# A ring of 64 pairs of gathered tiles in place of 32, laid over queries and table, with the experts' weights loaded after the gathers

## The chip, the core and the metric

The kernel runs on one core of one Trainium2 chip. Its engines are PE (matrix products), DVE and ACT (element by element), POOL (here mostly the issuer of indirect DMAs) and SP (here the issuer of plain DMAs and a counter of semaphores). The metric is device time in microseconds (us), lower is better. Of each kernel one further execution was profiled; all times inside the kernel come from it.

## What is computed

One layer over a graph of 6,250 nodes with 256 features and 206,250 edges (src, dst), sorted by dst. The parts that matter here, cut from the reference:

```python
x = h @ W                                   # 256 -> 64
el, er = x @ Wl.T, x @ Wr.T                 # 4 heads each
e = exp(leaky_relu(el[src] + er[dst], 0.2))
rowsum = segment_sum(e, src)
heads = [segment_sum((e / rowsum[src])[:, hd:hd+1] * x[dst], src) for hd in range(4)]
gnn = elu(stack(heads, axis=1) + b).reshape(N, 256)

x = x + gnn + linear_attention(layernorm(x))   # x here is the layer's input
x = x + moe(layernorm(x))                      # 8 experts, top 2, each 256 -> 256 -> 256
```

## The kernel before

Nodes are laid out in 49 tiles of 128. The kernel has four stages.

**Projections and sort.** PE and ACT project every tile to queries (q_all), keys, values and a row of the gather table tb (four er values, 64 features and a one: GW = 69 words). SP stores tb to HBM as gather_table. DVE meanwhile sorts all edges by src in SBUF; the attention runs beside the sort, and POOL adds its result to base in four chunks. At the end dst_x holds the sorted edges' dst and src_f their src.

**The edge loop.** The sorted edges form 806 pairs of tiles (NP; GT = 2 tiles of 128 edges in a pair). Nodes are cut into 196 windows of 32, and an item is a pair seen from one window. Items number 1,001, in groups of four: 251 groups (NG). DVE works out tables of which pair and window each item has, ACT sends them through HBM into registers' reach (trow), and every engine then runs a loop, four groups to a turn, with the pair and the window read into registers.

- POOL (lines 1548 to 1558) isn't looped: for every pair p it waits until pair p - 8 has been told ready (LAND = 8) and, from p = RING on, until pair p - RING is free, then issues two indirect DMAs, each of which gathers 128 rows of 276 bytes into gat.
- SP (watch, lines 1624 to 1637) goes through the pairs in order. It waits until pair p has landed and raises s_ready (L1627); then, from p = BEHIND on, it waits until the group that last uses pair p - BEHIND has been aggregated (s_agg) and raises s_free (L1636). With RING = 32, LAND = 8, BEHIND = 24 the same step of SP serves both of POOL's waits.
- ACT locates group g (L1392, waits for s_ready), copies the turned one-hots of group g - 1 from PSUM to hotT (L1382, waits for PE) and takes the exponential of group g - 3 (L1376).
- DVE makes one-hots (L773), sums and slopes the logits of group g - 2 (L754 to L768), weighs the one-hots of group g - 3 (L778) and adds up group g - 5 (L789).
- PE aggregates group g - 4 with 16 products from gat (L1145), spreads el of group g - 1 (L1135) and turns the one-hots of group g (L1127).

In its first eight groups ACT also issues load_expert: two DMAs of 256 KB each for one of the eight experts, the weights w1_s and w2_s (L1368, L1369). After its last group it issues two loads of biases (L1425).

**After the loop.** SP waits for all sums and issues, for each of seven tile groups, 16 small copies (L1646) that permute acc into moved. DVE averages (L832 to L836), ACT's exp_low (L1430) follows, then ELU, a second layernorm and the routing.

**Experts.** PE, ACT and DVE run the two-layer experts over slots of 128 tokens. Both PE and DVE first wait for s_ew, the landing of all weights and biases.

SBUF's large tensor is the arena, in which stages lie over each other by word offsets: q_all at 0 and tb at A_TB = 6272; src and dst of the edges from A_E = 9653; the two key buffers and right of the sort from A_K = 12981 to A_END1 = 17973. In the edge loop gat lay at A_K (32 x 138 words) and share_w behind it at A_S; the experts' weights lie at 0 to A_B = 8192, so over q_all and part of tb, which were free by then; hotT lay at A_B.

Of the kernel before, what the change touches and what calls it, by code (L numbers as in the profile page):

```python
# [10 lines left out]
BF16 = mybir.dt.bfloat16  # L11

P = 128
# [109 lines left out]
def gps_layer(nc, x, src, dst, W, Wl, Wr, gnn_b, w_qkv, mem_kv, w_out, b_out, g_out, g_pre,  # L123
# [3 lines left out]
    HD, C = Wl.shape  # L127
    _, MH, MD, MEM = mem_kv.shape
    HID = MH * MD
    NE, _, F = w1.shape  # L130
    T = -(-N // P)
    TAIL = N - (T - 1) * P
    SCALE = float(MD) ** -0.5
    KC = D // P
# [19 lines left out]
    GT = 2  # L154
    WN = 32
# [5 lines left out]
    GS = GI * GT  # L161
    NG = -(-NI // GI)
    RING, LAND, BEHIND = 32, 8, 24
    HOTS, UNROLL = 4, 4
    GW = HD + C + 1
    AW = C + 1
    SPL = 3 * HD + 1
# [16 lines left out]
    with ExitStack() as ctx:  # L184
        def sb(name, shape, dt=F32):
            return ctx.enter_context(nc.sbuf_tensor(name, shape, dt))
# [33 lines left out]
        A_E = A_TB + T * GW  # L220
        A_K = A_E + 2 * n_sort
        A_END1 = A_K + 3 * n_sort
        A_W1, A_W2 = 0, NE * KC * F
        A_B = A_W2 + NE * KC * D
        A_F = A_B + 2 * NE * D
        A_END2 = A_F + 2 * TS * RW + 12 * D
        A_G = A_K
        A_S = A_G + RING * GT * GW
        arena = sb("arena", [P, max(A_END1, A_END2, A_S + 2 * GS * P)])
# [8 lines left out]
        w1_s = arena[:, A_W1:A_W2].rearrange("p (e k f) -> p e k f", e=NE, k=KC)  # L238
        w2_s = arena[:, A_W2:A_B].rearrange("p (e k f) -> p e k f", e=NE, k=KC)
# [9 lines left out]
        assert A_F <= A_G  # L249

        spare = arena[:, A_END1:A_S + 2 * GS * P]
# [3 lines left out]
        o_el = T * 6 + (KC + 1) * P  # L255
        el_all = spare[:, o_el:o_el + T * HD].rearrange("p (t h) -> p t h", t=T)
        el3 = spare[:, o_el + T * HD:o_el + T * HD + -(-T * SPL // 2)].bitcast(BF16)[:, 0:T * SPL].rearrange("p (t c) -> p t c", t=T)
        assert o_el + T * HD + -(-T * SPL // 2) <= A_S + 2 * GS * P - A_END1
# [50 lines left out]
        gat = arena[:, A_G:A_S].rearrange("p (r w) -> p r w", r=RING)  # L309
        share_w = [x.rearrange("p (s h n) -> p s h n", s=GS, h=HD) for x in ring(A_S, 2, GS * P)]  # L310
        hot = [x.rearrange("p (s n) -> p s n", s=GS) for x in [rows_b.rearrange("p a c -> p (a c)").bitcast(BF16)[:, i * GS * WN:(i + 1) * GS * WN] for i in range(HOTS)]]
        hotT = [arena[0:WN, A_B + i * GS * P // 2:A_B + (i + 1) * GS * P // 2].bitcast(BF16).rearrange("p (c e) -> p c e", c=GS) for i in range(2)]
        assert A_B + GS * P <= A_E
# [51 lines left out]
        s_tab = sem("s_tab")  # L365
        s_ksub = sem("s_ksub")
        s_kexp = sem("s_kexp")
        s_qTp = sem("s_qTp")
# [4 lines left out]
        s_arow = sem("s_arow")  # L373
# [18 lines left out]
        s_agg = sem("s_agg")  # L392
        s_acc = sem("s_acc")
        s_ew = sem("s_ew")
# [869 lines left out]
        def _(act):  # L1264
# [98 lines left out]
            def load_expert(e):  # L1363

                if e == 0:
                    act.wait_ge(s_tab, 16)
                    act.wait_ge(s_qTp, T)
                act.dma_start(w1_s[:, e, :, :], w1[e].rearrange("(k p) f -> p k f", p=P)).then_inc(s_ew, 16)  # L1368
                act.dma_start(w2_s[:, e, :, :], w2[e].rearrange("(k p) f -> p k f", p=P)).then_inc(s_ew, 16)  # L1369

# [24 lines left out]
            def group(g, u):  # L1395

                now = g if isinstance(g, int) else NG // 2
                if u == 0:
                    values = items_of(act, "tile", g)
                    for v in range(UNROLL):  # L1400
                        place["tile", v] = values[v * GI:v * GI + GI]
                if now < NG:
                    locate(g, u)
                if 1 <= now < NG + 1:
                    copy_hot(g - 1, (u - 1) % UNROLL)
                if 3 <= now < NG + 3:
                    weights(g - 3, (u - 3) % UNROLL)
                if isinstance(g, int) and g < NE:
                    load_expert(g)
            assert NE <= 2 * UNROLL  # L1410
# [11 lines left out]
            for g in range(NG, NG + 3):  # L1422
                group(g, g % UNROLL)
            for rows, d in ((b1_b, b1), (b2_b, b2)):
                act.dma_start(rows.rearrange("p e f -> p (e f)"), d.rearrange("e f -> (e f)").partition_broadcast(P)).then_inc(s_ew, 16)  # L1425
# [85 lines left out]
        def _(pool):  # L1511
# [34 lines left out]
            pool.wait_ge(s_tab, 16)  # L1546

# [174 lines left out]
```

## Time and profile before

| | us |
|---|---|
| three runs | 3670.96, 3671.51, 3678.86 (median 3671.51) |
| profiled execution | 3671.64 |
| its span, first to last instruction | 3669.9 |
| first gather starts | 633.7 |
| last gather starts | 3069.8 |
| last aggregation ends | 3115.8 |

The span and the time of the profiled execution differ by 1.7 us. In the views an engine's busy time is that of its own instructions; DMAs that it issues, register loads and semaphore waits don't count. PE's matrix products and PEld's weight loads overlap. Where a view names a releaser, it is inferred from semaphore events; "remote" and "another core or an unknown queue" mean that none was found, and "issue" means time in which the engine waited for nothing that the profile shows. POOLq, SPq and ACTq are the engines' own instruction queues. The granted clock (PEclk) is a share of 2.4 GHz.

### The profile page before, as it was taken

How to read it: one execution, taken by the hardware profiler on the slowest of the kernel's cores; microseconds unless marked ns; L12 is line 12 of the kernel's file. 1: busy time of each engine (PE TensorE's matmuls, PEld its weight loads, DVE VectorE, ACT ScalarE, POOL GpSimd, SP SyncE). 2: the span in 40 equal slices, each digit the busy share in tenths (PEclk: the TensorE clock that was granted, in tenths of full speed). 3: DMA queues.
4: the chain of work that ended last, by engine and by line, in shares of the span. 5: the costliest groups of instructions: out<-in, count | busy, mean ns of one | idle time of the engine just before them, and what ended most of it. 6: DMA issues, size and time to landing. Idle time of an engine off the chain costs nothing.

```text
span 3669.9 us, 48930 instructions
## 1 busy us (share of the span) xinstructions
PE 1914.9 (52%) x10823; PEld 1641.5 (45%) x10824; DVE 1677.2 (46%) x5067; ACT 918.6 (25%) x2670; POOL 1845.4 (50%) x1844
## 2 busy tenths in 40 slices
PE   3824551154554455545555455545554557358874
PEld 1423331054544445444444444545444446247663
DVE  6788899233333333333333333333333334764343
ACT  3711221121211122112121112112121212564431
POOL 0021133666666666666666666666666662144433
PEclk9856655555555555555555555555555555569997
DMA  8020000211111111111111111111111111224554
GB/s 268 0 21 0 1 0 2 58 41 24 23 24 24 24 23 23 24 24 23 24 23 24 23 24 23 24 24 23 24 23 24 22 24 36 67 92 152 156 161 136
DMA packets 146361, 161.17 MB, mean 44 GB/s; under 512 B 44070, under 2 KB 113818, under 8 KB 146016
## 3 DMA queue, kind: packets, MB, share of 16 engines
q0 software_dynamic: 60992, 82.75, 11.5%
q1 hardware_dynamic: 79668, 70.58, 6.6%
q10 hardware_dynamic: 5612, 6.86, 0.6%
q8 instruction: 29, 0.48, 0.1%
q14 instruction: 60, 0.49, 0.0%
HBM read 101.18 MB, written 52.20 MB: 42 GB/s over the span
## 4 chain that ended last, share of the span: by engine, by line
another core or an unknown queue 42%; PE 21%; DVE 14%; issue 10%; ACT 7%; ACTq 2%; SPq 1%; POOL 1%; DVEq 1%; DMA 1%; POOLq 0%
PE ps L1145 6%; DVE arena L643 5%; DVE arena L642 4%; PE ps L1127 3%; ACT loc L1392 3%; PE ps L1223 3%; PE ps L1239 2%; ACT arena L1382 1%; PE ps L1104 1%; PE ps L1135 1%; ACTq L1392 1%; PE ps L1037 1%; PE ps L1231 1%; DVE arena L660 1%
## 5 line engine op out<-in xcount | busy, mean ns | idle before, releaser
L1557 POOL DMA_INDIRECT arena<-gather_table,arena x1612 | 1524.9, 946 | 928.5 <-issue 436.1
L1145 PE MATMUL ps<-arena 128*128 x4016 | 931.4, 419 | 208.5 <-issue 164.6
L1145 PEld LDWEIGHTS ps<-arena 128*128 128x128 f32 x4016 | 883.3, 329 | 263.5 <-issue 263.2
L1382 ACT ACTIVATE arena<-ps 32x1024 bf16<-32x1024 bf16 x251 | 254.0, 1012 | 1899.6 <-remote 1679.7
L778 DVE TENSOR_TENSOR arena<-rows_b,ps 128x1024 f32<-128x1024 bf16 x251 | 305.6, 1218 | 696.0 <-ACT ps L1376 546.9
L1135 PE MATMUL ps<-el,arena 32*128 x2008 | 115.4, 173 | 964.5 <-ACT arena L1382 843.5
L1135 PEld LDWEIGHTS ps<-el,arena 32*128 32x128 bf16 x2008 | 92.3, 102 | 1001.2 <-issue 981.3
L754 DVE TENSOR_REDUCE zed<-ps 128x32 f32<-128x96 f32 x251 | 64.2, 256 | 826.3 <-remote 756.8
L1127 PE MATMUL ps<-ident_b,rows_b 128*32 128x128 bf16 x2008 | 258.0, 310 | 26.6 <-issue 25.1
L643 DVE TENSOR_TENSOR arena<-arena 128x512 f32<-128x512 f32 (+2 forms) x328 | 248.1, 756 | 0.0
L789 DVE TENSOR_TENSOR big<-ps,big 128x65 f32 x1004 | 226.1, 225 | 46.7 <-issue 5.8
L1392 ACT ACTIVATE loc<-arena,xnx 128x2 f32 x1004 | 212.0, 280 | 105.1 <-issue 82.4
L1569 POOL DMA_INDIRECT slot_rows<-big,el x98 | 106.7, 1088 | 249.7 <-DVE ends_w L925 126.3
L1127 PEld LDWEIGHTS ps<-ident_b,rows_b 128*32 128x32 bf16 x2008 | 193.2, 139 | 37.5 <-issue 25.9
L642 DVE TENSOR_TENSOR arena<-arena 128x512 f32<-128x512 f32 (+2 forms) x328 | 205.3, 626 | 0.6
L1104 PE MATMUL ps<-ident,arena 128*128 128x128 f32 x286 | 61.0, 397 | 218.1 <-DVE arena L643 215.8
L1580 POOL DMA_INDIRECT arena<-expert_rows,el x98 | 93.4, 953 | 141.0 <-DMA expert_rows<-arena 67.7
L760 DVE TENSOR_TENSOR zed<-zed,arena 128x8 f32<-128x8 f32 x1004 | 156.8, 169 | 7.0 <-DVE zed L754 0.3
L1104 PEld LDWEIGHTS ps<-ident,arena 128*128 128x128 f32 x286 | 53.4, 211 | 227.2 <-DVE arena L643 223.2
L1223 PE MATMUL ps<-arena,xnx 128*128 x476 | 131.6, 401 | 22.7 <-issue 14.2
L1239 PE MATMUL ps<-arena 128*128 x476 | 127.1, 391 | 0.0
L1531 POOL TENSOR_TENSOR big<-big,xnx 128x896 f32<-128x896 f32 x7 | 15.7, 2272 | 217.3 <-DVE xnx L582 217.3
(269 smaller groups left out, 2187.1 us busy)
## 6 DMA issues: line engine op xcount, KB each, us to landing
arena<-gather_table,arena POOLq DMA_INDIRECT x1612
arena<-slot_rows SPq DMA_DIRECT2D x119, 128.0 KB
expert_rows<-arena SPq DMA_DIRECT2D x119, 128.0 KB
slot_rows<-ends_w SPq DMA_DIRECT2D x2, 4480.0 KB, 25.7
arena<-big SPq DMA_DIRECT2D x112, 56.9 KB
slot_rows<-ends_w SPq DMA_DIRECT2D x1, 6272.0 KB, 32.9
base<-in_x_dram SPq DMA_DIRECT2D x4, 1536.0 KB
out_dram<-base SPq DMA_DIRECT2D x5, 896.0 KB
```

Of the source, the lines that this page charges most:

```text
L642: dve.tensor_tensor(bl, al, ah, ALU.min if up else ALU.max).then_inc(s_key, 1)
L643: dve.tensor_tensor(bh, al, ah, ALU.max if up else ALU.min).then_inc(s_key, 1)
L778: dve.tensor_tensor(share_w[u % 2], bcast(hot[u % HOTS], 2, HD), bcast(pw, 3, WN), ALU.mult).then_inc(s_share, 1)
L789: dve.tensor_tensor(acc[:, bass.ds(b, 1), :], ps[:, 4 + par:5 + par, i * AW:i * AW + AW], acc[:, bass.ds(b, 1), :], ALU.add).then_inc(s_ac ...
L1127: ins = pe.transpose(out_[:, c * P:c * P + P], hot[u % HOTS][:, c, :], ident_b[:, :])
L1135: ins = pe.matmul(ps[:, 2 + par, c * SPL:(c + 1) * SPL], hotT[par][:, c, :], el4[0:WN, bass.ds(place["el", u][c // GT], 1), :].rearrange(" ...
L1145: ins = pe.matmul(ps[:, 4 + par, i * AW:i * AW + AW], share_w[par][:, i * GT + c, :, :].rearrange("p h n -> p (h n)"), gat[:, bass.ds(plac ...
L1223: ins = pe.matmul(ps[:, 1 + j % 2, 0:F], slot_T[j % 2][:, k, :], w1_s[:, bass.ds(e, 1), k, :].rearrange("p a f -> p (a f)"), start=(k == 0 ...
L1239: ins = pe.matmul(ps[:, 4 + j % 2, 0:D], hidT[j % 2][:, k * P:k * P + P], w2_s[:, bass.ds(e, 1), k, :].rearrange("p a f -> p (a f)"), star ...
L1382: act.activation(hotT[par], ps[0:WN, par, :].bitcast(BF16).rearrange("p (c e) -> p c e", c=GS), ACT.Copy).then_inc(s_hT, 1)
L1392: ins = act.activation(loc[u % 2][:, i * GT:i * GT + GT], src_f[:, bass.ds(place["tile", u][i], GT)], ACT.Identity, bias=bases[:, sl(g * G ...
L1557: pool.indirect_dma_start(gat[:, p % RING, c * GW:(c + 1) * GW], None, table_d, bass.IndirectOffsetOnAxis(ap=dst_x[:, t:t + 1], axis=0)).t ...
```

## The change

RING goes from 32 to 64 and BEHIND from 24 to 56; LAND stays 8. gat moves to the start of the arena, where q_all and tb lay (64 x 138 = 8,832 words, up to A_E at most). share_w moves to A_K, hotT behind it. Since the ring now lies where the experts' weights go, ACT's loads of them leave the first eight groups and stand behind a new wait for the last aggregation, ahead of the biases. POOL's gathers get one more wait, s_arow for all 49 tiles, since q_all is read until then. The early small tensors get their own room behind A_END1.

```diff
-    RING, LAND, BEHIND = 32, 8, 24
+    RING, LAND, BEHIND = 64, 8, 56
...
-        A_G = A_K
-        A_S = A_G + RING * GT * GW
-        arena = sb("arena", [P, max(A_END1, A_END2, A_S + 2 * GS * P)])
+        A_G = 0
+        A_S = A_K
+        N_SPARE = T * 6 + (KC + 1) * P + T * HD + -(-T * SPL // 2)
+        assert A_G + RING * GT * GW <= A_E and A_S + 3 * GS * P <= A_END1
+        arena = sb("arena", [P, max(A_END1 + N_SPARE, A_END2)])
...
-        gat = arena[:, A_G:A_S].rearrange("p (r w) -> p r w", r=RING)
+        gat = arena[:, A_G:A_G + RING * GT * GW].rearrange("p (r w) -> p r w", r=RING)
...
-            def load_expert(e):
-
-                if e == 0:
-                    act.wait_ge(s_tab, 16)
-                    act.wait_ge(s_qTp, T)
-                act.dma_start(w1_s[:, e, :, :], w1[e].rearrange("(k p) f -> p k f", p=P)).then_inc(s_ew, 16)
-                act.dma_start(w2_s[:, e, :, :], w2[e].rearrange("(k p) f -> p k f", p=P)).then_inc(s_ew, 16)
-
...
-                if isinstance(g, int) and g < NE:
-                    load_expert(g)
-            assert NE <= 2 * UNROLL
...
             for g in range(NG, NG + 3):
                 group(g, g % UNROLL)
+            act.wait_ge(s_agg, NG)
+            for e in range(NE):
+                act.dma_start(w1_s[:, e, :, :], w1[e].rearrange("(k p) f -> p k f", p=P)).then_inc(s_ew, 16)
+                act.dma_start(w2_s[:, e, :, :], w2[e].rearrange("(k p) f -> p k f", p=P)).then_inc(s_ew, 16)
...
             pool.wait_ge(s_tab, 16)
+            pool.wait_ge(s_arow, T)
```

## Rows read from the trace of the kernel before

**Rows 1.** The page's first part: each engine's busy time, share and instructions.
```profile
PE 1914.9 (52%) x10823; PEld 1641.5 (45%) x10824; DVE 1677.2 (46%) x5067; ACT 918.6 (25%) x2670; POOL 1845.4 (50%) x1844
```

**Rows 2.** Instructions of one line: ns min/median/max, first and last start in us.
```profile
L1557 POOL DMA_INDIRECT arena<-gather_table,arena x1612: 938/944/2112, 633.7 to 3069.8; - x180
...
L1368 ACTq DMA_DIRECT2D arena<-in_L_ffn_w_dram x8: 374/374/440, 668.7 to 759.6; - x8
```

**Rows 3.** The chain that ended last, 3070 to 3130: start us, us, what.
```profile
3096.51 3.61 PE ps L1145 x16
...
3101.39 3.61 PE ps L1145 x16
...
3105.30 10.45 PE ps L1145 x48
...
3117.23 0.57 SPq L1646
...
3126.72 2.02 DMA arena<-big
```

**Rows 4.** The list of waits: engine line, releaser: us in total, times, longest.
```profile
ACT arena L1382 <- remote: 1679.7, 166, 24.6
...
POOL arena L1557 <- SPq L1627: 400.8, 142, 16.8
...
POOL arena L1557 <- SPq L1636: 73.7, 35, 3.6
```

**Rows 5.** The list of waits of SP's own queue.
```profile
SPq L1636 <- remote: 1702.3, 154, 17.1
```

**Rows 6.** Who waited for SP's line 1627: us in total, times.
```profile
  ACT loc L1392: 17.9, 22
```

**Rows 7.** Copies of L1382 by stretch: stretch, its length, ACT busy (count), PEclk, DMA, GB/s.
```profile
633.00:785.00 152.00, 9.09 (x9) 0.50 0.24 55
785.00:1785.00 1000.00, 103.44 (x103) 0.50 0.14 24
3070.80:3120.00 49.20, 7.08 (x7) 0.50 0.13 48
```

**Rows 8.** Gathers of L1557 by stretch, the same columns with POOL's busy time.
```profile
633.00:785.00 152.00, 96.82 (x98) 0.50 0.24 55
785.00:1785.00 1000.00, 624.47 (x662) 0.50 0.14 24
```

**Rows 9.** Timeline, 1510 to 1540, of ACT and of POOL.
```profile
1513.15 1.01 ACT L1382 ACTIVATE arena<-ps 32x1024 bf16<-32x1024 bf16 x1 [17.66 <-remote]
...
1522.84 1.01 ACT L1382 ACTIVATE arena<-ps 32x1024 bf16<-32x1024 bf16 x1 [3.47 <-remote]
...
1539.02 1.01 ACT L1382 ACTIVATE arena<-ps 32x1024 bf16<-32x1024 bf16 x1 [14.30 <-remote]
...
1513.98 0.94 POOL L1557 DMA_INDIRECT arena<-gather_table,arena  x1 [3.49 <-SPq L1627]
...
1537.14 0.94 POOL L1557 DMA_INDIRECT arena<-gather_table,arena  x1 [0.31 <-issue]
```

**Rows 10.** Timeline, 670 to 736, of ACT and of POOL.
```profile
670.76 1.01 ACT L1382 ACTIVATE arena<-ps 32x1024 bf16<-32x1024 bf16 x1
...
710.40 1.01 ACT L1382 ACTIVATE arena<-ps 32x1024 bf16<-32x1024 bf16 x1 [31.89 <-issue]
...
725.89 1.01 ACT L1382 ACTIVATE arena<-ps 32x1024 bf16<-32x1024 bf16 x1 [13.18 <-remote]
...
734.48 0.94 POOL L1557 DMA_INDIRECT arena<-gather_table,arena  x1 [16.81 <-SPq L1627]
```

**Rows 11.** Timeline of ACT after the loop.
```profile
3133.54 1.70 ACT L1430 ACTIVATE arena<-big 128x1792 f32<-128x1792 f32 x1 [24.92 <-DVE big L836]
```

**Rows 12.** All engines by stretch: PE, PEld, DVE, ACT, POOL busy, PEclk, DMA, GB/s.
```profile
3108.00:3116.00 8.00, 7.73 (x37) 7.54 (x36) 3.38 (x11) 0.20 (x1) 0.00 (x0) 0.50 0.67 262
3300.00:3400.00 100.00, 86.70 (x467) 72.19 (x468) 39.84 (x128) 48.23 (x122) 42.38 (x44) 0.97 0.46 152
```

More of the change, by code:

```diff
@@ L248, in gps_layer @@
         back = [arena[:, A_F + i * 2 * D:A_F + (i + 1) * 2 * D].rearrange("p (c d) -> p c d", c=2) for i in range(2 * TS * RW // (2 * D))]
-        assert A_F <= A_G
-        spare = arena[:, A_END1:A_S + 2 * GS * P]
+        spare = arena[:, A_END1:A_END1 + N_SPARE]
         stats = spare[:, 0:T * 6].rearrange("p (t s) -> p t s", t=T)
@@ L257, in gps_layer @@
         el3 = spare[:, o_el + T * HD:o_el + T * HD + -(-T * SPL // 2)].bitcast(BF16)[:, 0:T * SPL].rearrange("p (t c) -> p t c", t=T)
-        assert o_el + T * HD + -(-T * SPL // 2) <= A_S + 2 * GS * P - A_END1
         CQ = 2 * HD + C
@@ L308, in ring @@
             return [arena[:, start + i * width:start + (i + 1) * width] for i in range(n)]
-        gat = arena[:, A_G:A_S].rearrange("p (r w) -> p r w", r=RING)
+        gat = arena[:, A_G:A_G + RING * GT * GW].rearrange("p (r w) -> p r w", r=RING)
         share_w = [x.rearrange("p (s h n) -> p s h n", s=GS, h=HD) for x in ring(A_S, 2, GS * P)]
         hot = [x.rearrange("p (s n) -> p s n", s=GS) for x in [rows_b.rearrange("p a c -> p (a c)").bitcast(BF16)[:, i * GS * WN:(i + 1) * GS * WN] for i in range(HOTS)]]
-        hotT = [arena[0:WN, A_B + i * GS * P // 2:A_B + (i + 1) * GS * P // 2].bitcast(BF16).rearrange("p (c e) -> p c e", c=GS) for i in range(2)]
-        assert A_B + GS * P <= A_E
+        hotT = [arena[0:WN, A_S + 2 * GS * P + i * GS * P // 2:A_S + 2 * GS * P + (i + 1) * GS * P // 2].bitcast(BF16).rearrange("p (c e) -> p c e", c=GS) for i in range(2)]
         ident_b = sb("ident_b", [P, P], BF16)
```

## The prediction

> **What bounds the kernel now.** Read the page's first part before anything else: over the span no engine is busy for much more than half of it [rows 1], so the time is in waits. The edge loop (251 groups, 806 pairs of gathered tiles, so 3.21 pairs to a group) holds some 2,400 of the 3,670 us, from the first gather at 633.7 us to the last aggregation at 3105.30 + 10.45 = 3115.8 us [rows 2, 3]. The list of waits says who waits there [rows 4 to 6]. Three things are to be seen in it. First, the consumer is never short of data: ACT's localisation, the step that needs a landed pair, waited 17.9 us in all. Second, the producer is held back by the ring: POOL waited 400.8 + 73.7 = 474.5 us for SP's two counters, and SP itself waited 1702.3 us at L1636 for an aggregation of the pair 24 behind. Third, ACT waited 1679.7 us ahead of its copy of the turned one-hots (L1382), for a releaser that the profile can't name.
>
> The counts by stretch give the pace [rows 7, 8]: 103 groups in 1,000 us are 9.7 us a group, and 662 gathers (331 pairs) in the same 1,000 us. POOL alone could do a gather in 0.94 + 0.31 = 1.25 us [rows 9], 2.5 us a pair, 8.03 us a group. After the last gather (started 3069.8) the same loop runs at 3101.39 - 3096.51 = 4.88 us a group [rows 2, 3]. So neither the consumer's own work (4.88) nor the gathers' issue (8.03) sets 9.7. The timeline shows what does [rows 9]. POOL resumes at 1513.98; ACT's copies follow at 1522.84, and then none until 1539.02, 0.9 us after POOL's last gather of that run ended (1537.14 + 0.94). The copy at 1513.15 came after 17.66 us of idleness, and POOL had stood for 3.49 us when it resumed at 1513.98. The pattern is that the consumer all but freezes while POOL issues without a pause and comes back when POOL is stopped, and what stops POOL is the full ring. I know no mechanism for this and argue from the pattern alone.
>
> **What the change does, step by step.**
>
> *A ring of 64.* In the state where the ring is full, the pairs issued equal the ring plus the pairs freed. By 785 us 98 gathers, 49 pairs, are issued [rows 8], 49 - 32 = 17 are freed, 5.3 groups, while 9 groups are copied [rows 7]: copies run 3.6 groups ahead of frees. A deeper ring takes no step out of the cycle. In steady state it is full again, POOL gets credit only as the consumer frees it, and I take the pace to stay at 9.7. What moves are the two ends of the loop.
>
> At the end the last 64 pairs are drained without gathers beside them, not the last 32: 32 / 3.21 = 10 more groups at 4.88 in place of 9.7, a gain of 48.2 us.
>
> At the start POOL runs on after 717.7 us, where it stopped before (16.81 us ahead of 734.48 [rows 10]). With N groups copied when the ring fills, this happens at 717.7 + 2.5 x (32 + 3.21 x (N - 3.6)) us = 797.7 + 8.03 x (N - 3.6). Before, N groups were copied by 785 + 9.7 x (N - 9). The difference, the delay, is 71.1 - 1.67 x N us. N hangs on the consumer's pace p under an unbroken stream of gathers, counted from the third copy at 725.9. The nearest row is the start itself: copies at 670.76, 710.40 and 725.89 [rows 10], two groups in 55.1 us, so p = 27.6. That gives N = 6.4, a full ring at 820 us, a delay of 60.4 and a net of +12. The one bound: no further group passes, N = 3, where the difference from the real 725.9 is 67.0, net +19. The other bound, the frozen interval in the middle of the loop, 1539.02 - 1522.84 = 16.2 us [rows 9]: N = 11.2, delay 52.4, net +4. Below p = 14.3 (N = 13.7) the sign turns; at the steady 9.7 nothing is lost at the start and the full 48 us are gained. I take +12, since the start of the loop has the same unbroken stream.
>
> *Where the ring lies.* Gathers now also wait for all 49 attention tiles; POOL's own additions to base, which stand before them on its queue, already need every one of those tiles, so the wait costs nothing and holds up nobody. The gather's rows, sizes and count are the same, and so are the table steps: zero. hotT and share_w only change address: zero, within one instruction of the same form.
>
> *SP's watch.* It now waits for an aggregation from pair 56 on, not 24. Readiness is therefore told without a stop for 56 pairs, so POOL's second limit (8 pairs past the last ready one) doesn't bind early and the ring is really deeper. The register loads of the released groups are as many, less four: zero.
>
> *The experts' weights.* Sixteen issues of about 0.37 us (L1368's [rows 2]; L1369's are alike in size) leave ACT's first eight groups, some 6 us. There ACT is idle between copies by 13 us and more [rows 10] and POOL sets when the ring fills, so I take 0, at most -7. They move behind the last aggregation at 3115.8 us and hold ACT until about 3123 with the two bias loads behind them. Who is queued behind is exp_low(0), which started at 3133.54 after 24.92 us of idleness [rows 11]: 10 us of cover are left; without it the cost would be the issues' 6 to 7 us. The weights themselves, 16 x 256 KB = 4.2 MB, at the 262 GB/s of the stretch in which the biases land [rows 12], need 16 us, and PE and DVE first want them in the expert stage, behind six passes over tile groups. But SP issues its sixteen permuting copies at the same moment, from 3117.23 until the last lands at 3126.72 + 2.02 = 3128.7 [rows 3], and these are on the path: DVE starts on them. No row shows the two queues side by side. Bounds: nothing; or 7 us of issue plus 3 us for the 768 KB of weights ahead of SP's first copy, 10. I take +3, near the low end, since SP's sixteen issues outlast ACT's and a copy is small beside the 4.2 MB.
>
> The Trainium skill ("Perfetto Trace Analysis", DMA Instruction — HWDGE) says that the descriptor hardware is locked for one issuer at a time and that the profile's span of an issue holds the lock's wait. By it SP's sixteen issues would stretch by ACT's, +7 in place of +3, 3690 us in all in place of 3686. No row of this trace shows two such queues at once.
>
> **Sum.** 12 + 0 + 3 = +15 us. The profiled execution took 3671.64 us (span 3669.9, 1.7 us around it), 0.1 us over the median of 3671.51. So 3671.5 + 15 = 3686.5 us; I say 3686.
>
> **The rivals.**
>
> *The consumer keeps its pace under the stream (faster).* If the long freezes are the ring's doing and not the stream's, the extra 32 pairs are gathered beside a consumer at 9.7 us, and only the fast drain remains: -48 + 3, 3626 us. For it: the copies of 1513.15 and 1522.84 are 9.7 us apart with POOL running between them [rows 9]. Against it: the copy of 710.40, 39.6 us after the one before, when POOL's ring wasn't full yet [rows 10].
>
> *POOL's waits go away (much faster).* If the deeper ring takes up all 474.5 us of waiting, less the usual 0.3 us at each of 142 + 35 places, the last gather comes 421 us earlier, and the drain of 20 groups in place of 10 is 49 us longer: 3671.5 - 421 + 49 + 3 = 3303 us. For it: the waits are real, and the gathers' floor is 8.03 us a group. Against it: the consumer would have to hold 8.03 us under an unbroken stream, where the only stretch seen gave 27.6.
>
> *Start and end cancel.* At p near 14.3 the loop is as long as before: 3671 to 3676 us. For it: p is read from two groups, during which ACT also issued weights, which this change removes.
>
> *The clock.* In the drain PE was busy 7.73 of 8 us at a granted 0.50, 1.2 GHz; in a later stage the granted clock was 0.97, near 2.4 GHz [rows 12]. If a drain twice as long got the fast level for its last 10 groups, with PE's 3.61 us of aggregation [rows 3] at half, some 20 us would come off: 3666 us. The Trainium skill ("TensorE: Matmul & The Clock Gate", Part 1) says that sustained activity releases the clock; the trace disagrees for this mix of instructions, which stayed at 0.50 through the whole drain [rows 7].
>
> *The weights collide (slower still).* The high bound of the end stage and N = 3, +10 + 19, give 3700 us; if the first stop of POOL, 16.81 us [rows 10], comes again at the full ring, its excess over 3.49 us adds 13: 3713 us.
>
> **How the numbers follow.** The forecast's own case 0.46 (3675 to 3700 us), slower still 0.12, cancelling 0.18, the consumer's steady pace 0.11, the clock 0.05, POOL's waits gone 0.08. About 0.2% (7.3 us) is what a measurement of this kernel can tell from no change. Slower by more: 0.46 less the 0.06 of it under 3679, plus 0.12, 0.52. Within: 0.18 + 0.06 + 0.05 - 0.04 = 0.25. Faster: 0.11 + 0.08 and the edge of the cancelling case and the clock's, 0.04: 0.23. The range reaches from 3630 to 3715 us: it holds the forecast, the slower and the cancelling case and the clock's, and leaves out the two gains, 0.19.
>
> **What would show it.** In the profile after: POOL's gathers unbroken from 633.7 us to about 820 us, with some 70 to 75 pairs issued; six or seven copies at L1382's place by then, not twelve; in the middle still about 103 groups in 1,000 us, and POOL's waits about as long in total; 73 pairs issued at 820 and 733 more at 3.02 us end the gathers near 3034 us, 36 us earlier than before; then a drain of 19 groups at 4.88 us, to 3128 us in place of 3115.8. SP's sixteen issues still about 0.63 us apart; exp_low not later than DVE's second step. The prediction is wrong if the middle's pace differs from 9.7 by over 0.1 us, which alone moves the end by 23 us, or if the groups copied by 820 us are over 13.

## The result and the profile after

The kernel after the change took 3739.98 us in the median of four runs (3721.15, 3738.22, 3741.75, 3742.40), the kernel before 3675.19 us beside it (3670.96, 3671.51, 3678.86, 3693.67). The ratio is 1.0142, 95% interval 1.0099 to 1.0185: slower by some 1.4%, where 3686 us was forecast. The profiled execution took 3738.22 us (span 3736.5), 66.6 us more than that of before.

The engines' totals say little, as the first line of the page of the kernel after shows: every entry is within 30 us of [rows 1].

```profile
PE 1943.4 (52%) x10823; PEld 1660.6 (44%) x10824; DVE 1665.6 (45%) x5067; ACT 918.4 (25%) x2670; POOL 1850.2 (50%) x1844
```

So the span is cut at three marks: the first gather, the last gather, the end of the last aggregation. The gathers' line gives the first two (as [rows 2]: ns min/median/max, first and last start), the chain the third.

```profile
L1550 POOL DMA_INDIRECT arena<-gather_table,arena x1612: 942/947/2118, 657.3 to 3079.7; - x180
```

```profile
3166.26 10.45 PE ps L1144 x48
```

| stretch | before | after | difference |
|---|---|---|---|
| start to first gather | 633.7 | 657.3 | +23.6 |
| first gather to last gather | 2436.1 | 2422.4 | -13.7 |
| last gather to end of last aggregation | 46.0 | 97.0 | +51.0 |
| behind that, and around the span | 555.8 | 561.5 | +5.7 |

The first row lies ahead of the edge loop, where the change adds only POOL's wait for s_arow; e1 below has its first gather as late (657.7) without that wait. The other three rows are the change: +43.0 us.

**The start of the loop.** ACT's copies of the turned one-hots, and the last of POOL's unbroken gathers with the first one behind its stop (timeline; in brackets the idle time ahead):

```profile
694.35 1.01 ACT L1373 ACTIVATE arena<-ps 32x1024 bf16<-32x1024 bf16 x1 [0.84 <-issue]
734.00 1.01 ACT L1373 ACTIVATE arena<-ps 32x1024 bf16<-32x1024 bf16 x1 [37.89 <-issue]
778.80 1.01 ACT L1373 ACTIVATE arena<-ps 32x1024 bf16<-32x1024 bf16 x1 [43.04 <-remote]
822.90 1.01 ACT L1373 ACTIVATE arena<-ps 32x1024 bf16<-32x1024 bf16 x1 [40.80 <-issue]
839.25 1.01 ACT L1373 ACTIVATE arena<-ps 32x1024 bf16<-32x1024 bf16 x1 [14.47 <-remote]
...
820.49 0.95 POOL L1550 DMA_INDIRECT arena<-gather_table,arena  x1 [0.31 <-issue]
839.82 0.95 POOL L1550 DMA_INDIRECT arena<-gather_table,arena  x1 [18.38 <-SPq L1620]
```

Three groups are copied by the time the ring is full (821.4 us, 164.1 us after the first gather; 84.0 in the kernel before). The distances are 39.6, 44.8 and 44.1 us, and the fourth copy comes 1.5 us after POOL has stopped. The gathers issued up to the first stop, in the kernel before (L1557) and in the kernel after (L1550; POOL busy and count, then PEclk, DMA, GB/s), are exactly the ring's 32 and 64 pairs, so nothing was freed in time to prolong the run:

```profile
633.00:717.70 84.70, 64.75 (x64) 0.50 0.25 52
```

```profile
657.30:821.40 164.10, 125.37 (x128) 0.50 0.19 31
```

The cut of one long interval shows where its time goes (timeline, 734 to 782 us; POOL's gathers, one each 1.25 us, are left out):

```profile
735.15 0.58 PE L1134 MATMUL ps<-el,arena 32*128 x8 [38.08 <-ACT arena L1373]
...
735.79 1.01 PE L1126 MATMUL ps<-ident_b,rows_b 128*32 128x128 bf16 x8
756.40 0.26 DVE L753 TENSOR_REDUCE zed<-ps 128x32 f32<-128x96 f32 x1 [43.04 <-issue]
```

PE's `el` products end at 735.73, and DVE, which waits for them, starts 20.7 us later. PE's turn of the one-hots ends at 736.80, and ACT's copy, which waits for it, starts at 778.80, 42 us later. In between only DVE works, for 1.7 us from 756.40. What is late is the handover itself, while POOL issues a gather each 1.25 us. Not every handover is late: SP went on telling pairs ready through this gap (738.87, 740.47, 742.92 us and so on), 1.6 to 2.5 us behind the end of each pair's gathers.

**The middle and the drain** (copies of L1373 by stretch; columns as in [rows 7]):

```profile
657.30:821.40 164.10, 3.04 (x3) 0.50 0.19 31
1000.00:2000.00 1000.00, 104.48 (x103) 0.50 0.15 24
3081.00:3176.00 95.00, 16.22 (x16) 0.50 0.00 1
```

There are 103 groups in 1,000 us, as before [rows 7], and 16 copies in the drain where there were 7, at a clock of 0.50 throughout. POOL's and ACT's waits stayed nearly as long (list of waits; compare [rows 4]; POOL's second wait, for L1629, adds 15.7 us in the kernel after, so 450.8 in place of 474.5):

```profile
ACT arena L1373 <- remote: 1604.1, 151, 43.0
...
POOL arena L1550 <- SPq L1620: 435.1, 152, 18.4
```

**Behind the loop.** DVE's first step on the permuted sums, in the kernel before and in the kernel after:

```profile
3128.84 0.18 DVE L832 TENSOR_SCALAR el<-arena 128x28 f32<-128x28 f32 x1 [11.39 <-DMA arena<-big]
```

```profile
3194.62 0.18 DVE L831 TENSOR_SCALAR el<-arena 128x28 f32<-128x28 f32 x1 [16.20 <-DMA arena<-big]
```

Of the kernel after, the issues of ACT's weights (first of the two lines) and of SP's copies (ns min/median/max, first and last start):

```profile
L1414 ACTq DMA_DIRECT2D arena<-in_L_ffn_w_dram x8: 450/524/1333, 3176.7 to 3185.9; - x8
...
L1639 SPq DMA_DIRECT2D arena<-big x112: 507/591/1192, 3178.2 to 3295.0; - x112
```

DVE waits 4.8 us longer for the copies that SP issues. SP's first sixteen issues, those beside ACT's, took 9.70 us together where they took 9.43, and the sixteenth started 9.76 us behind the first where it was 9.49; ACT's weight issues beside them rose from 0.374 us [rows 2] to 0.524, some to 1.33. From the sixteenth issue's start to DVE's first step it is 6.7 us (3187.96 to 3194.62) where it was 2.1.

### The profile page after: what moved, and what is told of

It reads as the page before. It is cut to its first block, busy times and chain, and to the rows that moved or that the text cites. A ratio compares the mean times of both kernels' runs of the same rounds, so it can differ in the third digit from the quotient of the medians.

```text
span 3736.5 us, 48845 instructions
## 1 busy us (share of the span) xinstructions
PE 1943.4 (52%) x10823; PEld 1660.6 (44%) x10824; DVE 1665.6 (45%) x5067; ACT 918.4 (25%) x2670; POOL 1850.2 (50%) x1844
## 4 chain that ended last, share of the span: by engine, by line
another core or an unknown queue 39%; PE 22%; DVE 16%; issue 13%; ACT 6%; SPq 2%; ACTq 2%; DVEq 1%; DMA 1%; POOL 1%; POOLq 0%
PE ps L1144 6%; DVE arena L642 5%; DVE arena L641 4%; PE ps L1126 3%; PE ps L1222 3%; PE ps L1238 2%; ACT loc L1383 2%; PE ps L1103 1%; ACT arena L1373 1%; PE ps L1134 1%; PE ps L1036 1%; PE ps L1077 1%; ACTq L1383 1%; PE ps L1230 1%
## 5 line engine op out<-in xcount | busy, mean ns | idle before, releaser
L1550 POOL DMA_INDIRECT arena<-gather_table,arena x1612 | 1529.1, 949 | 910.6 <-issue 442.5
L1373 ACT ACTIVATE arena<-ps 32x1024 bf16<-32x1024 bf16 x251 | 254.6, 1014 | 1940.8 <-remote 1604.1
L1126 PE MATMUL ps<-ident_b,rows_b 128*32 128x128 bf16 x2008 | 258.0, 309 | 27.6 <-issue 25.3
L759 DVE TENSOR_TENSOR zed<-zed,arena 128x8 f32<-128x8 f32 x1004 | 146.5, 166 | 2.5 <-issue 0.2
L1523 POOL TENSOR_TENSOR big<-big,xnx 128x896 f32<-128x896 f32 x7 | 15.7, 2275 | 218.7 <-DVE xnx L581 218.7
```

The costliest lines, as they stand in the source:

```text
L1126: ins = pe.transpose(out_[:, c * P:c * P + P], hot[u % HOTS][:, c, :], ident_b[:, :])
L1373: act.activation(hotT[par], ps[0:WN, par, :].bitcast(BF16).rearrange("p (c e) -> p c e", c=GS), ACT.Copy).then_inc(s_hT, 1)
L1550: pool.indirect_dma_start(gat[:, p % RING, c * GW:(c + 1) * GW], None, table_d, bass.IndirectOffsetOnAxis(ap=dst_x[:, t:t + 1], axis=0)).t ...
```

## The experiments

The runs went to five chips, A to E, each in one session; the kernels of one group of rows below ran on one chip. All variants carry one addition, a mask on the two values that ACT and SP load and wait against, so on chip A they are compared with the masked kernel before (e1) first:

```diff
-                    act.wait_ge(s_ready, place["tile", u][GI - 1] + 2)
+                    act.wait_ge(s_ready, (place["tile", u][GI - 1] & 4095) + 2)
...
-                    sp.wait_ge(s_agg, done[0][u])
+                    sp.wait_ge(s_agg, done[0][u] & 4095)
```

"Loop" is from the first gather to the end of the last aggregation, "drain" its part behind the last gather's start, both from the profiled execution; the ratio is to the kernel before on the same chip.

| chip, its kernel before | run | median us | ratio, 95% | first gather | loop | drain | behind |
|---|---|---|---|---|---|---|---|
| A, 3675.96 | e1 before, masked | 3690.64 | 1.0024 (0.9996-1.0052) | 657.7 | 2490.2 | 46.8 | 554.1 |
| | e2 64 slots, depth 32 | 3661.91 | 0.9929 (0.9901-0.9958) | 657.4 | 2443.7 | 47.8 | 557.0 |
| | e3 64 slots, depth 48 | 3665.71 | 0.9965 (0.9937-0.9994) | 641.3 | 2466.2 | 80.7 | 556.5 |
| | e4 32 slots, depth 24 | 3634.37 | 0.9878 (0.9829-0.9928) | 634.7 | 2434.5 | 32.4 | 553.9 |
| B, 3198.30 | e5 32 slots, new place | 3209.40 | 1.0039 (1.0006-1.0071) | 633.3 | 2038.2 | 22.8 | 520.6 |
| | e6 depth 20 | 3214.90 | 1.0021 (0.9991-1.0051) | 656.9 | 2038.2 | 22.9 | 519.6 |
| | e7 pause | 3608.24 | 1.1279 (1.1216-1.1341) | 641.7 | 2451.8 | 22.3 | 515.6 |
| | e8 one gather a pair | 2551.62 | | 636.9 | 1394.6 | 45.7 | 517.6 |
| C, 3680.02 | e9 after, masked | 3727.04 | 1.0133 (1.0066-1.0199) | 639.7 | 2521.6 | 97.2 | 555.4 |
| | e10 32 slots, new place | 3700.09 | 1.0036 (1.0006-1.0065) | 641.8 | 2492.0 | 46.0 | 560.7 |
| | e11 pause | 3646.56 | 0.9902 (0.9872-0.9933) | 658.0 | 2451.8 | 22.3 | 552.8 |
| | e12 one gather a pair | 2693.96 | | 657.9 | 1479.1 | 47.7 | 555.2 |
| D, 3200.90 | e13 tiny pause | 3273.03 | 1.0228 (1.0182-1.0275) | 633.3 | 2114.8 | 22.8 | 517.7 |
| | e14 pause each 4 | 3309.41 | 1.0328 (1.0276-1.0380) | 634.5 | 2142.2 | 22.8 | 514.5 |
| | e15 64 slots, pause | 3623.05 | 1.1309 (1.1241-1.1377) | 658.4 | 2451.6 | 22.2 | 519.8 |
| E, 3718.07 | e16 after, masked | 3755.43 | 1.0096 (1.0066-1.0125) | 657.1 | 2556.6 | 101.8 | 561.0 |
| | e17 tiny pause | 3717.06 | 0.9998 (0.9968-1.0027) | 657.8 | 2521.1 | 45.9 | 552.0 |
| | e18 pause each 4 | 3722.69 | 0.9996 (0.9968-1.0023) | 643.3 | 2514.9 | 45.5 | 557.8 |

**First set (chip A): depth.** The theory: depth alone is the loop's loss, through the unbroken gathers that fill the ring. Rivals: the ring's place, the late weights.

> The kernel before with one thing added: the values that ACT and SP wait against in the edge loop pass through a mask (and 4095), one register operation more for each group on ACT and for each pair on SP. All the variants below carry the same mask, so this is what they are compared with. If the mask is cheap (0.05 us on ACT, off the path on SP): loop from first gather to last aggregation 2482 us as before, at most 10 us more. Two theories differ on the 23.6 us by which the changed kernel was later already at its first gather. Luck of the granted clock in the sort stage: executions of this kernel, too, come with the first gather near 634 us or near 657 us, and totals fall into two heaps some 20 us apart. An effect of the change: all stay near 634.

The loop came to 2490.2, 8 us over the 2482 of before. I took this for the mask's price, but the times on one chip don't tell it from nothing (1.0024, 0.9996 to 1.0052), and the masked kernel after (e9) is only 2 us over the kernel after. Its first gather was at 657.7. The windows of 300 to 320 us show why the sort stage has two lengths (PE, PEld, DVE, ACT, POOL busy, PEclk, DMA, GB/s). The kernel before:

```profile
300.00:320.00 20.00, 15.24 (x128) 14.97 (x127) 18.05 (x41) 6.58 (x6) 0.00 (x0) 0.93 0.00 1
```

e1, the same code but for the mask:

```profile
300.00:320.00 20.00, 20.00 (x96) 20.00 (x94) 14.14 (x28) 6.36 (x3) 0.00 (x0) 0.50 0.01 1
```

The kernel after:

```profile
300.00:320.00 20.00, 20.00 (x96) 20.00 (x95) 14.15 (x28) 6.36 (x3) 0.00 (x0) 0.50 0.00 1
```

At a granted 0.93 PE did 128 instructions, at 0.50 (1.2 GHz) 96, and DVE, which waits for them, falls behind. e13, the same code again up to the loop, had 0.93 here and its first gather at 633.3. In all twenty profiles the two go together: 0.85 to 0.93 in this stretch with a first gather at 633 to 643 us (eleven), 0.50 with one at 657 to 658 (nine). So the 23.6 us are luck of the execution and no effect of the change, and both kernels come either way. Compared like with like, 3721 against 3671 to 3679 and 3738 to 3742 against 3694, the change costs some 47 us, 1.3%; the profiles gave 43.

> The changed kernel with BEHIND 24 in place of 56: its ring keeps its place and its 64 slots, the weights stay late, but POOL is held 32 pairs ahead at most. Theory A, depth is the whole loss: the loop (first gather to last aggregation) falls from 2519 us to that of the kernel before, 2482 within 5, the drain from 97 to 46 us, and what stays is the 5.7 us behind the loop. Theory B, the loss comes from the ring's new place or the late weights: the loop stays near 2519.

```diff
-    RING, LAND, BEHIND = 64, 8, 56
+    RING, LAND, BEHIND = 64, 8, 24
```

Neither theory held: the drain fell to 47.8 us as depth 32 demands, but the loop to 2443.7, 46 us under e1. Something in this kernel beyond depth makes it faster (e10 narrows it down). Behind the loop it is 2.9 us over e1.

> The changed kernel with BEHIND 40: depth 48. Theory A, the fill of the ring costs in proportion to its depth (37.3 us for 32 pairs, 1.17 us a pair): loop 2482 + 19 = 2501 us, drain 71 us, ring full 124 us after the first gather. Rival C, a threshold (the consumer is stopped at all depths over 32 by about the same): 2519 us at depth 48 as well.

This is the same line with BEHIND 40. The loop took 2466.2 us instead of 2501, by the same unforeseen gain; but against e2 it is 22.5 us more for 16 pairs, 1.4 us a pair, and POOL first stopped 126.6 us after the first gather (124 expected). So there is no threshold at 32.

> The kernel before with BEHIND 16 in place of 24: 8 slots of its ring are never used ahead, depth 24. Theory A: the same line goes on below 32, 8 x 1.17 = 9.4 us less, loop 2473 us, drain 34 us, and this would beat both kernels. Rival D, the consumer runs out of landed pairs at a shallow depth (it holds some 5 groups, 16 pairs, at once): ACT's localisation waits for readiness over 100 us in all in place of 18, and the loop is longer than 2482.

This is the kernel before with BEHIND 16. It is faster than both kernels, 1.2% under before. Its loop is 9.2 us under e2's for 8 pairs, 1.15 a pair. Rival D's sign is there and its consequence isn't (waits of e4):

```profile
ACT loc L1392 <- SPq L1627: 777.0, 175, 10.8
```

ACT now waits 777 us for readiness, and the loop is shorter all the same: the waits have moved from one handover to another.

**Second set (chip B).** Here the kernel before took 3198.30 us, 13% less than on chip A.

> The changed kernel with 32 slots and BEHIND 24, with the mask: ring in its new place, late weights, POOL's added wait, depth 32, and like the kernel before no slot to spare (slots = BEHIND + LAND). The run with 64 slots and depth 32 gave a loop of 2443.7 us, 46 us less than the masked kernel before (2490.2), which depth alone doesn't explain. Theory E, spare slots do it (POOL is then held by one counter, readiness, and never by the second, the freed slots): without spare slots the loop is back at 2490 within 6. Rival F, the new place, the added wait or the late weights do it: the loop stays near 2444. In both cases the part behind the loop is 2 to 6 us longer than 554.1.

> The kernel before with the mask, BEHIND 16 and LAND 4: depth 20, 12 slots spare. Depth 24 with LAND 8 gave a loop of 2434.5 us. Theory A (a pair less of depth is 1.17 us less, in the fill alone): 2430 us, the first stop of POOL 53 to 56 us after its first gather. Rival D (too little landed ahead): POOL stops more often, the pace in the middle rises over 9.57 us a group, loop over 2440.

> The kernel before with the mask and a small fill of a scratch tile (512 elements a partition) on POOL ahead of each pair, which POOL waits for: its gathers then come in twos with a gap of about 0.5 to 1 us, and never in an unbroken run. Theory G, the freeze needs gathers without any gap: the long intervals between ACT's copies (over 12 us) all but vanish, and the pace in the middle is POOL's own, about 3.2 x (2.5 + gap). Rival H, the freeze follows POOL being at work at all, or its wait on another counter: the long intervals stay, and the pace rises over 9.7 us a group by what the gaps add, up to 3 us.

> The kernel before with the mask and only the first of the two gathers of each pair: the second tile of each pair is not gathered (old contents are used in its place). POOL's own pace for a group is then 3.21 x 1.25 = 4.0 us, under the consumer's 4.88. Theory G/H, POOL's issuing freezes the consumer and each stop lets it take a few groups: POOL reaches the full ring in half the time, the first full ring is about 41 us after the first gather, and the pace in the middle falls to about 4.0 us plus the stops (1.9 us), near 6 us a group. Rival I, the consumer alone is slow for a reason of its own (DVE, PE and ACT handing over): the pace stays near 9.7.

e5 is the changed kernel with `RING, LAND, BEHIND = 32, 8, 24`; e6 the kernel before with `32, 4, 16`. Both had a loop of 2038.2 us, which no expectation named. The gathers' line and the first copies of e5:

```profile
L1550 POOL DMA_INDIRECT arena<-gather_table,arena x1612: 940/944/2112, 633.3 to 2648.7; - x180
```

```profile
670.28 1.01 ACT L1373 ACTIVATE arena<-ps 32x1024 bf16<-32x1024 bf16 x1 [0.84 <-PE ps L1126]
673.04 1.01 ACT L1373 ACTIVATE arena<-ps 32x1024 bf16<-32x1024 bf16 x1 [1.00 <-PE ps L1126]
675.78 1.01 ACT L1373 ACTIVATE arena<-ps 32x1024 bf16<-32x1024 bf16 x1 [0.98 <-PE ps L1126]
```

1612 gathers in 2015.4 us is one each 1.25 us from first to last: POOL never stopped. Under the same unbroken stream, with gathers of the same length (944 ns against 947), the copies stand 2.8 us apart where they stood 39.6. On this chip there is no freeze (so I call the late handovers under the stream), and the ring never fills at depth 20 or 32. The pause of e7 (its edit is shown at e11) then only costs: 9.70 us a group. e8, which leaves out the second gather of each pair, ran at 5.40 us a group; there POOL stopped at a full ring again, so this is the consumer's pace beside the stream and not POOL's.

**Third set (chip C, with freezes).**

> The changed kernel with the mask. Two kinds of chip have been seen: on one the kernel before takes 3676 us and the consumer freezes while POOL gathers; on the other it takes 3198 us, POOL's 1612 gathers run without one stop (2015.4 us), and kernels of depth 20 and 32 have the same loop, 2038.2 us. Theory J, depth costs only where the chip freezes the consumer: on a freezing chip the loop is 2519 + 8 = 2527 us and the ratio to before about 1.017 to 1.02; on the other the loop is 2038 within 2, and only the late weights remain, 1 to 6 us, ratio 1.000 to 1.003. Rival K, the deeper ring or its place costs on any chip: a loop over 2050 us on the other chip too.

This is theory J's case for a chip with freezes: loop 2521.6 us (2527 expected), drain 97.2. Against e10, the same code with 32 slots and depth 32 on the same chip, it is 29.6 us for 32 pairs.

> As e5, which came to a chip without freezes and told nothing of the spare slots. On a freezing chip: theory E, spare slots are what made depth 32 faster: without them the loop is 2490 within 8 and the ratio to before 1.002 to 1.004; rival F, the new place, POOL's added wait or the late weights are: the loop is 2444 within 8, ratio near 0.993. On the other chip: 2038 again.

Theory E holds: 2492.0, not 2444. e10 and e2 have the same BEHIND, place, weights and waits and differ in the slots alone, 32 and 64. So the new place and the late weights cost the loop nothing (e1: 2490.2), and spare slots gain some 48 us. Both comparisons are between chips A and C, whose kernels before differ by 4 us. The waits of e2 and of e10 show it as shorter stops of POOL, 441 us in all against 491:

```profile
POOL arena L1550 <- SPq L1620: 366.7, 161, 16.7
...
POOL arena L1550 <- SPq L1629: 74.3, 67, 3.3
```

```profile
POOL arena L1550 <- SPq L1620: 404.0, 145, 16.8
...
POOL arena L1550 <- SPq L1629: 86.9, 60, 3.6
```

By the code, POOL is held by readiness alone where slots are spare, and is one pair further ahead: it issued 66 gathers before its first stop in e2 and 64 in e10. (That e2's list names L1629 at all is the view's inference.) Why this makes more and shorter stops I can't say.

> As e7, which came to a chip without freezes (gap of 0.81 us between pairs, loop pace 9.70 us, of POOL's making alone). On a freezing chip: theory G, the freeze needs gathers without a gap: pace again 9.7 to 9.8 us a group, copies at even distances of 9 to 12 us. Rival H, the gap of 0.5 us more doesn't let the others through: the long intervals stay and the pace is POOL's 9.7 plus the stops' 1.7 to 1.9, 11.5 us, loop near 2880 us.

```diff
+                pool.memset(idle[:, :], 0.0).then_inc(s_idle, 1)
+                pool.wait_ge(s_idle, p + 1)
                 for c in range(GT):
```

```profile
1506.08 0.94 POOL L1561 DMA_INDIRECT arena<-gather_table,arena  x1 [0.30 <-issue]
1507.02 0.54 POOL L1557 MEMSET idle<- 128x512 f32 x1
1507.83 0.95 POOL L1561 DMA_INDIRECT arena<-gather_table,arena  x1 [0.27 <-POOL idle L1557]
```

```profile
L1561 POOL DMA_INDIRECT arena<-gather_table,arena x1612: 940/949/2229, 658.0 to 3087.6; - x180
```

Theory G holds. With 0.81 us between two pairs in place of 0.31 the freezes are gone on a chip that has them. The whole loop, 2451.8 us, is that of e7 on chip B to the tenth; in the loop's run copies stand 8.9 to 12.3 us apart, POOL never stopped, the drain is 22.3 us. Though POOL does 0.5 us more for each pair, the loop is 38 us shorter than e1's.

> As e8 (only the first gather of each pair; the second tile is not gathered), which on the chip without freezes ran at 5.40 us a group, the consumer's own pace. On a freezing chip, if the freeze lasts as long as POOL issues: each group costs POOL's 3.21 x 1.25 = 4.0 us plus what the consumer needs of its own with POOL stopped, about 4 to 5 us a group as in the drain where it can't be overlapped, 6 to 9 us a group in all. If the freeze comes from the number of descriptors rather than from POOL being busy, the freezes also halve in length: intervals between copies over 12 us become intervals of 6 to 9.

The pace is 5.70 us a group against 5.40 on chip B. Of the 250 distances between copies 31 are over 8 us, the longest 10.7; in e8 none is (longest 6.9), in the kernel before 85 are over 12 and make up 1565 us. So the freezes are there and short. Between the two readings of the expectation this doesn't decide.

**Fourth and fifth set (chips D without, E with freezes): how much of a gap.** e13 and e17 fill 8 elements in place of 512. e14 and e18 have the pause of e11 ahead of each fourth pair only. e15 has the pause in the changed kernel.

> The kernel before with the mask and a pause of POOL ahead of each pair, as in e11, but with a fill of 8 elements a partition in place of 512: the gap between two pairs is then an instruction and its wait, an estimate of 0.4 to 0.6 us in place of 0.81. Theory G1, any break in the stream lets the others through: no long intervals between copies, no stop of POOL, pace 3.21 x (2.5 + 0.1 to 0.3) = 8.4 to 9.0 us a group, loop 2100 to 2260 us, total 3300 to 3450 us on a freezing chip. Theory G2, the gap must have some length: long intervals come back in part, pace over 9 us.

> The kernel before with the mask and the pause of e11 (512 elements, gap 0.81 us) ahead of each fourth pair only: the stream has a break each 10 us. Theory G1, the others stand still in between and catch up in a break: 0.8 us isn't enough for a group's chain of handovers (4.9 us), so long intervals stay, POOL stops at the full ring, pace 9.0 to 9.8. Theory G3, what is broken by any pause is a state that must build up over tens of us: no long intervals, POOL's pace of 3.21 x (2.5 + 0.5 / 4) = 8.4 us a group, loop 2116 us.

> The changed kernel with the mask and the pause of e11 ahead of each pair. Theory A, depth costs only through the freeze at the start: with the pause the ring never fills, and the loop is that of e11 (gathers 2429.6 us, drain under 25 us) though the ring is 64 deep; total that of e11 plus 1 to 6 us for the late weights. Rival, the deeper ring costs by itself: loop 30 us or more longer than e11's.

On chip D nothing froze, so these gave only POOL's own pace: 8.35 and 8.46 us a group. e15's loop, with 64 slots and depth 64, is e7's within 0.2 us: where the stream is broken and the ring never fills, depth costs nothing (shown on a chip without freezes only).

> The changed kernel with the mask, again (e9). On a freezing chip a repetition: loop 2520 +- 8 us, drain 97 us, ratio 1.013 to 1.02. On a chip without freezes, where it hasn't run yet: theory J, depth costs nothing there: loop 2038 within 2, ratio 1.000 to 1.004; rival K, the ring's depth or place costs there too: loop over 2050 us.

On chip E the kernel before takes 3718 us, some 40 more than on A and C, and I don't know why. The loop took 2556.6 us, over the 2512 to 2528 expected, and the drain 101.8. The changed kernel at depth 64 never came to a chip without freezes unless with the pause (e15), so theory J rests on e5, e6 and e15 there.

> As e13 (8 elements; the gap between two pairs is 0.39 us there in place of 0.31, pace 8.35 us a group), which came to a chip without freezes. On a freezing chip: theory G1, any instruction between the gathers that POOL's engine works on lets the others through: pace 8.35 to 8.5, no stops, total near 3300 us. Theory G2, it is the length of the gap: 0.39 us is hardly more than 0.31, the freezes are as before, pace 9.7 or more, total 3680 to 3760 us.

> As e14 (0.81 us gap ahead of each fourth pair, pace 8.46 us a group on a chip without freezes). On a freezing chip: theory G1/G2, the others stand still for the 10 us between two gaps: intervals between copies come in multiples of about 10 us, POOL stops at the full ring, pace 9.0 to 10. Theory G3, a short gap each 10 us is enough to keep the freeze from setting in: pace 8.5, no stops, total near 3310 us.

```profile
695.80 1.01 ACT L1384 ACTIVATE arena<-ps 32x1024 bf16<-32x1024 bf16 x1
721.79 1.01 ACT L1384 ACTIVATE arena<-ps 32x1024 bf16<-32x1024 bf16 x1 [23.91 <-remote]
750.02 1.01 ACT L1384 ACTIVATE arena<-ps 32x1024 bf16<-32x1024 bf16 x1 [26.15 <-remote]
```

Theory G2 holds for e17 (the lines are its first copies), and G1 and G2 for e18. A gap of 0.39 us ahead of each pair leaves the freezes (26 and 28 us at the start where the kernel before had 39.6, then a pace of 9.9); so does a gap of 0.81 ahead of each fourth pair (pace 9.9). Both are level with the kernel before, and e17 has 87 distances over 12 us, 1562 us in all, much as that has (85, 1565 us). So at each pair 0.81 us is enough and 0.39 is not, though the first was seen on chip C and the second on chip E. Whether it is the length of the gap that frees the consumer or the lower rate of gathers that comes with it (a pair each 3.0 us in e11, each 2.6 in e17) these runs don't separate.

## Why the prediction was wrong

*Direction and mechanism: right.* The pace in the middle stayed (103 groups in 1,000 us, forecast 103), POOL's waits stayed, the clock stayed at 0.50 in the longer drain, ring, table and waits cost nothing themselves (e10 against e1: 2492.0 and 2490.2), and the loss is made while the ring fills. That depth is the cause is shown on the chips that freeze: e4, e2 and e3 with spare slots, e10 and e9 without.

*The step that failed: p, the consumer's pace under an unbroken stream.* I took 27.6 us, the mean of 39.6 and 15.5 [rows 10]. The second interval wasn't under the stream: POOL had stopped at 717.7, 8.2 us before its copy. The stretch had one clean interval, 39.6, and the change shows 44.8 and 44.1 behind it. With N = 3 the formula gives +67.0, which I had as the bound. The measured delay at the full ring is 71.9: the third copy of the kernel before came 92.2 us after the first gather, and the ring of the kernel after was full, with three copies made, at 164.1.

The 5 us more are the formula's own error. It took 3.6 groups of lead from 785 us, where 17 pairs had been freed, back to a full ring at N = 3, where it gives 62 pairs issued; the trace has 64, none freed, and 32 in the kernel before. So the fill simply takes 32 x 2.5 = 80 us longer (164.1 against 84.0). From the full ring to the ninth copy it was then 60.5 us, against 55.9 from the third to the ninth before: 4.6 more, of which POOL's first stop, 18.38 us against 16.81, is 1.6. That is far from the +13 of the last rival, since the kernel before has such a stop as well. Measured in all: the ninth copy comes 224.6 us after the first gather instead of 148.1, +76.5.

*The drain's gain was too large.* I had ten more groups at 4.88 us, -48.2. There were nine more (16 copies against 7) for 51.0 us, 5.7 each: the copies of the drain stand 4.9 us apart and each fourth 6.4 to 6.9, 5.4 on average, and my 4.88 was the short distance alone. The remaining 2.4 us lie at the drain's first copies. Nine groups at 9.7 less 51.0 is -36.3. With the start, +40.2; measured for the loop +37.3, the rest lying in the middle.

*Behind the loop: 5.7 us for 3.* This is within the bounds 0 and 10. SP's issues account for 0.3 us of it; the rest of DVE's 4.8 us is the time to the landing of SP's copies. That the weights' data lay ahead of them is argued, not shown. The Trainium skill ("Perfetto Trace Analysis", DMA Instruction — HWDGE) would have had SP's issues stretched by the lock; the sixteen beside ACT's took 9.70 us together where they took 9.43, so they hardly were, and ACT's were (0.374 to 0.524 us in the median). Over all profiles the part behind the loop is 4.1 us longer with the late weights on chips that freeze (558.4 against 554.3 us, six and seven kernels) and 3.2 us on the others (520.2 against 517.0, two and five); kernels of one kind differ among themselves by up to 6 us.

*The sum.* +76.5 - 36.3 - 3 + 5.7 = +43 for the change, where I had +15. The other 23.6 us of the profiled difference are the sort stage's clock, which no step named: the three runs shown of before lay within 8 us and gave no sign of a second length. The clock alone doesn't excuse the miss: the one run of the kernel after without that delay took 3721.15 us, still over a range that reached to 3715. The range failed because its upper end stopped at a case of 0.12 whose parts turned out to be the likeliest ones.

*The rivals.* The steady pace and the end of POOL's waits did not come on the chips that freeze; start and end did not cancel; the clock did not rise. "POOL's waits gone" is what chip B does without any change: no stop at all and a loop of 2038 us in e5 and e6, and 3198 us for the kernel before; chip D, with 3201, is alike.

*Left open.* What the freeze is. The traces show handovers between PE, ACT and DVE late by 20 and 42 us while SP's readiness steps came on time, gathers of unchanged length, and an effect of the gap between pairs. Loading of instructions isn't it: from 1000 to 2000 us the kernel before moved 8 packets of instructions and had 35 distances over 12 us between its copies, e5 moved 9 and had none. The Trainium skill ("SBUF — State Buffer", SBUF: two separate sides) says that only DVE and GpSimd share a port and that PE and ACT never wait on anyone there; the trace agrees in that ACT's copies, once started, take 1.01 us in the stream as in the drain; what held their start it doesn't say. Why some chips freeze and others don't, at the same granted clock and the same gathers, was not found; each chip was seen in one session only, so it may also hang on something of that session. Nor was the cause of the spare slots' gain found.

A kernel faster than both where it freezes is e4 (ratio 0.9878), and e6, shallower still, is level with before on a chip without freezes (1.0021, 0.9991 to 1.0051). The pause of e11 gains 1.0% where it freezes and costs 12.8% where it doesn't.

## What to carry to other kernels

A deeper ring helps only if the consumer is short of data or the producer's lead is used up; where the ring is full all the time and the consumer isn't waiting for data, find out first what stops the consumer, here by looking at what the producer does in each of the consumer's long gaps. To size a state that a change will make longer, use only the intervals that lie wholly inside it: one clean 39.6 was worth more than its mean with a 15.5 that the end of the state had cut short. Count what has been freed when a ring first fills; don't carry a lead back from a later stretch. Try slots to spare beyond the lead and a short lead, and measure on more than one chip before paying for a cure.

## What the runs showed of the hardware

- On three chips (and where the kernels before and after ran) an unbroken stream of POOL's indirect gathers, one each 1.25 us, held up handovers between PE, ACT and DVE by up to 42 us, while SP's steps for the same gathers came 1.6 to 2.5 us behind them; on two chips no profile had any of it, and the kernel before took 3198 and 3201 us against 3676 to 3718.
- Gathers took 944 to 947 ns in the median where it froze and 944 where it didn't. A gap of 0.81 us ahead of each pair of gathers removed the effect (chip C); 0.39 us, or 0.81 us each fourth pair, did not (chip E).
- The part behind the loop, too, took 515 to 521 us on the chips without freezes and 552 to 561 on the others; POOL issues 196 more indirect DMAs there.
- Over one stretch of 20 us in the sort stage TensorE's granted clock was 0.93 (mostly 2.4 GHz) or 0.50 (1.2 GHz) in executions of the same code, and some 20 us of the kernel's time went with it.
- In the drain PE was busy all of 20 us (3150 to 3170 us of the kernel after) at a granted 0.50.
